# Gathered edges of a graph layer: summed in chunks of 25 tiles through 128-column one-hots, or in units of 16 tiles through 32-column ones

## The reference

```python
h  = x @ node_w.T                       # 12500 x 64
rf = edge_attr_64 @ review_w.T          # 400000 x 64
m  = (h[src] + rf) * edge_weight1
x  = layernorm(x + segment_sum(m, dst, 12500))
```

## Time and profile before

| | before |
|---|---|
| median of 3 runs | 4755.46 us (4745.97 to 4756.59) |
| the profiled execution | 4764.11 us, of which the span from the first to the last instruction is 4762.4 us |
| granted TensorE clock, mean | 0.752 of full speed |
| TensorE busy | 2948.5 us (62%) |
| VectorE busy | 1864.9 us (39%) |
| GpSimd busy | 1996.9 us (42%) |
| ScalarE busy | 1005.4 us (21%) |
| DMA, mean | 39 GB/s |

### The profile page before, as it was taken

One profiled execution on the slowest core, in us unless ns is written; L12 is line 12 of the kernel. 1 busy time (PEld: TensorE's weight loads), 2 busy tenths in 40 slices (PEclk: granted clock), 3 DMA queues, 4 the chain that ended last, 5 costly groups with the idle time before them and its releaser, 6 DMA issues.

```text
span 4762.4 us, 69733 instructions
## 1 busy us (share of the span) xinstructions
PE 2948.5 (62%) x25313; PEld 2219.9 (47%) x25314; DVE 1864.9 (39%) x5496; ACT 1005.4 (21%) x1593; POOL 1996.9 (42%) x2023
## 2 busy tenths in 40 slices
PE   0666666566666666676567566567566576577565
PEld 0444454444444444454445444455355355355345
DVE  2444344334334344344344344344344244344344
ACT  0222122122122122122122122122122122122112
POOL 7334444444444444444444444443443433433541
PEclk9777777677777777777777777677678688677677
DMA  5111211111121211111211212111121111111121
GB/s 102 36 32 39 40 35 39 35 39 35 39 39 34 40 38 36 40 39 34 40 34 39 40 34 39 35 40 37 36 40 37 37 38 38 37 38 38 38 43 33
DMA packets 522588, 186.20 MB, mean 39 GB/s; under 512 B 483570, under 2 KB 490049, under 8 KB 522051
## 3 DMA queue, kind: packets, MB, share of 16 engines
q1 hardware_dynamic: 304936, 74.04, 8.2%
q0 software_dynamic: 64000, 65.66, 7.2%
q10 hardware_dynamic: 153302, 41.80, 4.0%
HBM read 178.15 MB, written 3.20 MB: 38 GB/s over the span
## 4 chain that ended last, share of the span: by engine, by line
PE 56%; another core or an unknown queue 22%; issue 16%; ACT 4%; DVE 2%; DVEq 0%; POOL 0%; ACTq 0%; POOLq 0%
PE count_ps L882 26%; PE x_sums_ps L897 17%; PE window_ps L840 10%; ACT counts L745 4%; DVE hot_lo L497 1%; PE attr_ps L874 1%; PE turn_ps L859 0%; PE turn_ps L856 0%; PE x_sums_ps L906 0%; PE x_sums_ps L905 0%; DVE scatter L442 0%; DVE hot_key L496 0%; DVE x_tab L550 0%; DVE x_tab L563 0%
## 5 line engine op out<-in xcount | busy, mean ns | idle before, releaser
L367 POOL DMA_INDIRECT rows<-x,src x2000 | 1988.2, 994 | 2673.1 <-DMA src<-src 2086.4
L882 PE MATMUL count_ps<-hot_key,hot_lo 128*128 128x343 bf16 x6750 | 1480.6, 373 | 1271.0 <-ACT counts L745 637.9
L882 PEld LDWEIGHTS count_ps<-hot_key,hot_lo 128*128 128x128 bf16 x6750 | 702.1, 115 | 1849.0 <-issue 1068.4
L745 ACT ACTIVATE counts<-count_ps 128x686 f32<-128x686 f32 x1125 | 896.5, 802 | 1952.9 <-remote 1090.7
L496 DVE TENSOR_SCALAR hot_key<-count,cols 128x686 bf16<-128x686 f16 x1125 | 467.3, 415 | 1696.7 <-remote 1031.9
L897 PE MATMUL x_sums_ps<-counts,x_tab 128*64 128x126 f32 (+1 forms) x12348 | 820.9, 282 | 365.7 <-issue 333.4
L897 PEld LDWEIGHTS x_sums_ps<-counts,x_tab 128*64 128x64 f32 x12348 | 732.3, 143 | 439.0 <-issue 395.3
L497 DVE SCALAR_TENSOR_TENSOR hot_lo<-count,cols 128x384 bf16<-128x384 f16 x1125 | 686.4, 610 | 0.0
L442 DVE TENSOR_SCALAR scatter<-column,dst_left,w 128x128 f32<-128x128 f32 x2000 | 523.0, 352 | 254.8 <-PE window_ps L840 237.4
L840 PE MATMUL window_ps<-scatter,rows 128*128 128x128 f32 x4000 | 490.4, 284 | 72.3 <-issue 61.6
L840 PEld LDWEIGHTS window_ps<-scatter,rows 128*128 128x128 f32 x4000 | 475.6, 199 | 92.2 <-issue 89.6
(11 more groups left out here) (112 smaller groups left out, 641.1 us busy)
## 6 DMA issues: line engine op xcount, KB each, us to landing
rows<-edge_attr SPq DMA_DIRECT2D x80, 800.0 KB
g_attr<-edge_attr ACTq DMA_DIRECT2D x62, 576.0 KB, 4.5
rows<-x,src POOLq DMA_INDIRECT x2000
out<-x_tab SPq DMA_DIRECT2D x11, 256.0 KB
counts<-dst SPq DMA_DIRECT2D x1, 1562.5 KB
src<-src SPq DMA_DIRECT2D x80, 12.5 KB, 1.7
dst<-dst SPq DMA_DIRECT2D x80, 12.5 KB
w<-edge_weight SPq DMA_DIRECT2D x80, 12.5 KB
```

Source lines behind the costliest of these rows:

```text
L367: pool.indirect_dma_start(out=rows[:, s, k, 0:F], out_offset=None, in_=x, in_offset=bass.IndirectOffsetOnAxis(ap=src_sb[s][:, k:k + 1].bit ...
L745: act.activation(counts[:, :, t * SPAN:(t + 1) * SPAN].rearrange("p (a h) d -> p a h d", a=2), count_ps[t % 2][:, :, 0:HALF].rearrange("p ...
L882: last = pe.matmul(count_ps[b][:, a, 0:HALF], hot_lo[h][:, i, :], hot_key[h][:, a * HALF:(a + 1) * HALF], start=(i == 0), stop=(i == 2))
```

## The change

Gathered edges are now worked in units of 16 tiles (2048 edges), and all that depends on the loop over windows is gone from the main path.

1. 116 units are gathered (1856 tiles), and 1269 tiles are counted, in 71 groups. A round has ten groups and sixteen units (`STEPS = (2, 1, 2, 1, 2, 2, 1, 2, 1, 2)`), there are seven rounds and no steps behind them, and the last four units stand where the last two chunks stood. The four slots of `rows` hold a unit each.
2. A tile's edges are laid along the partitions in their order. Its one-hot has the 7 nodes that a tile can span, padded to 32 columns, and is the stationary operand: 16 matmuls per unit (32 passes) put each tile's sums on a group of 32 partitions of `unit_ps`, four tiles side by side and four blocks along the bank. ScalarE copies `unit_ps` to SBUF, and four matmuls (8 passes) with a one-hot of 128 partitions x 128 nodes per block, which VectorE makes from each tile's first node, bring the unit into one window of 128 nodes. VectorE adds it at a base read from a table.
3. `src`, `dst` and the weights come in batches of 64 tiles, with a tile on a partition; VectorE subtracts each tile's first node, TensorE turns the batch (7 matmuls) in the middle of `sum_x`, and ScalarE and VectorE copy it. A gather waits for that copy and for the slot, and no longer for a load of its own.
4. A slot is freed by TensorE's last matmul of the unit's sums, and both SyncE's load and GpSimd's gather wait for that, where they waited for VectorE's add before.
5. VectorE's 25 one-hots of 128 x 128 per chunk become two operations of 128 x 112 and one of 128 x 512 per unit.
6. At the start four units (64 tiles) are gathered before the flag is known, where it was four chunks (100 tiles). The tables by chunk are made only where the flag says that all is to be gathered; a table by unit takes their place. The flag now asks the bound of 7 nodes of the gathered tiles too.

```diff
+UT = 16
+SLOTS = 4
+BATCH = 4
+CYCLE = 16
+UNITS = 116
+STEPS = (2, 1, 2, 1, 2, 2, 1, 2, 1, 2)
+LATE_UNITS = 4
+PAD = 32
...
+            def gather_unit(unit):
+                s, c = unit.i % SLOTS, unit.i // BATCH
+                pool.wait_ge(src_ready, unit.b + 1)
+                if not isinstance(unit.u, int) or unit.u >= SLOTS:
+                    pool.wait_ge(unit_summed, unit.u - SLOTS + 1 + BEGUN)
+                pool.sem_inc(gathers_begun, 1)
+                for t in range(UT):
+                    k = unit.i % BATCH * UT + t
+                    pool.indirect_dma_start(
+                        out=rows[:, s, t, 0:F], out_offset=None, in_=x,
+                        in_offset=bass.IndirectOffsetOnAxis(ap=src_cols[:, c, k:k + 1].bitcast(U32), axis=0),
+                    ).then_inc(gathered[s], 16)
...
+            def make_unit_hot(unit):
+                h, k = unit.i % 2, unit.i % BATCH * UT
+                dve.wait_ge(batch_read, unit.b + 1)
+                dve.wait_ge(unit_summed, unit.u - 1 + BEGUN)
+                hot = unit_hot[h][:, :, 0:SPAN]
...
+                dve.tensor_tensor(hot, column[:, 0:SPAN].unsqueeze(1).to_broadcast([P, UT, SPAN]), rel, ALU.is_equal
+                                  ).then_inc(unit_hot_made, 1)
+                dve.wait_ge(unit_hot_made, unit.u * 2 + 1)
+                dve.tensor_tensor(hot, hot, w, ALU.mult).then_inc(unit_hot_made, 1)
...
+            def copy_unit(unit):
+                act.wait_ge(unit_summed, unit.u + 1 + BEGUN)
+                act.wait_ge(unit_multiplied, unit.u - 1 + BEGUN)
+                act.activation(unit_slots[unit.i % 2][:, :], unit_ps[:, :], ACT.Copy).then_inc(unit_copied, 1)
...
+            def sum_unit(unit):
+                s, h = unit.i % SLOTS, unit.i % 2
+                pe.wait_ge(unit_hot_made, unit.u * 2 + 2)
+                pe.wait_ge(attr_landed[s], (unit.b + 1) * 16)
+                pe.wait_ge(gathered[s], (unit.b + 1) * (16 * UT))
+                pe.wait_ge(unit_copied, unit.u + BEGUN)
+                for b in range(BLOCKS_U):
+                    for j in range(QUADS):
+                        t = b * QUADS + j
+                        done = pe.matmul(unit_ps[j * PAD:(j + 1) * PAD, b * 2 * F:(b + 1) * 2 * F],
+                                         unit_hot[h][:, t, :], rows[:, s, t, :], start=True, stop=True)
+                done.then_inc(unit_summed, 1)
+            def multiply_unit(unit, before):
+                pe.wait_ge(unit_copied, unit.u + 1 + BEGUN)
+                pe.wait_ge(slot_hot_made, unit.u + 1)
+                pe.wait_ge(added, before)
+                for b in range(BLOCKS_U):
+                    done = pe.matmul(unit_window_ps, unit_slots[unit.i % 2][:, b * 2 * F:(b + 1) * 2 * F],
+                                     slot_hot[unit.i % 2][:, b, :], start=(b == 0), stop=(b == BLOCKS_U - 1))
+                done.then_inc(unit_multiplied, 1)
...
-                def step_of(g, chunks):
-                    until = sum_chunk(*chunks[0])
+                def step_of(at, turned_batch):
+                    g, units = at.g, at.units
+                    sum_unit(units[0])
                     turn_slots(g - 1)
-                    count_tiles(g)
-                    for chunk in chunks[1:]:
-                        until = sum_chunk(*chunk, until)
-                    multiply_slots(g - 1)
-                    sum_x(g)
+                    wait_attr(g)
+                    if turned_batch:
+                        pe.wait_ge(src_ready, turned_batch.q + 1)
+                    for n, from_ in enumerate(range(0, GT, 2 * HOT_BUFS)):
+                        count_tiles(g, range(from_, min(GT, from_ + 2 * HOT_BUFS)))
+                        if n < len(units):
+                            multiply_unit(units[n], at.added + n)
+                        if n + 1 < len(units):
+                            sum_unit(units[n + 1])
+                    multiply_slots(g - 1, at.added + len(units))
+                    sum_x(g, at.batch)
```

More of the change, by code:

```diff
@@ L21 @@
+from collections import namedtuple
 from contextlib import ExitStack
@@ L287, in round_steps @@
         def round_steps(r):
[L289 removed]
+            i, adds = 0, r * (CYCLE + ROUND_GROUPS) + 1
             for n, size in enumerate(STEPS):
[L291 to L305 removed]
+                units = [unit_at(r, k) for k in range(i, i + size)]
+                begun = [k // BATCH for k in range(i, i + size) if k % BATCH == 0]
+                batch = batch_at(r, begun[0] + 2) if begun else None
+                if isinstance(r, int) and batch and batch.q >= BATCHES:
+                    batch = None
+                yield Step(r * ROUND_GROUPS + n + 1, units, batch, adds)
+                i += size
+                adds += size + 1
@@ L663, in _, with step_of @@
                 begin_hot(1)
-                def step_of(g, chunks):
-                    until = add_chunk(*chunks[0])
-                    make_hot(g, range(HOT_BUFS, GT))
-                    for chunk in chunks[1:]:
-                        until = add_chunk(*chunk, until)
-                    add_slots(g - 1, until)
+                make_unit_hot(unit_at(0, 0))
+                def step_of(at, ahead):
+                    g, units = at.g, at.units
+                    make_slot_hot(units[0])
+                    make_hot(g, range(HOT_BUFS, 2 * HOT_BUFS))
+                    for unit in units[1:]:
+                        make_unit_hot(unit)
+                    make_hot(g, range(2 * HOT_BUFS, 3 * HOT_BUFS))
+                    for unit in units[1:]:
+                        make_slot_hot(unit)
+                    make_hot(g, range(3 * HOT_BUFS, 4 * HOT_BUFS))
+                    add_unit(units[0], at.added)
+                    make_hot(g, range(4 * HOT_BUFS, GT))
+                    for unit in units[1:]:
+                        add_unit(unit, at.added + 1)
+                    for unit in ahead:
+                        make_unit_hot(unit)
+                    if at.batch:
+                        prepare_batch(at.batch)
+                    add_slots(g - 1, at.added + len(units))
                     make_slots_hot(g)
@@ L971, in _ @@
                     multiply_out(early, 0, 1)
-                for c in range(CHUNKS - LATE_CHUNKS, CHUNKS):
-                    until = sum_chunk(*at_slot(c), until)
+                for n, unit in enumerate(last_units):
+                    sum_unit(unit)
+                    if n:
+                        multiply_unit(last_units[n - 1], last_adds + n)
+                multiply_unit(last_units[-1], last_adds + LATE_UNITS)
                 with pe.If(calm_now == 0):
```

633 lines of the change are left out of this document (439 added, 194 removed).

## The result

| | before | after |
|---|---|---|
| median of 4 runs | 4750.72 us (4744.17 to 4756.59) | 4394.43 us (4365.81 to 4404.48) |
| ratio | | 0.9232, 95% interval 0.9186 to 0.9278 |
| the profiled execution | 4764.11 us, span 4762.4 | 4404.48 us, span 4402.7 |
| granted TensorE clock, mean | 0.752 | 0.791 |

The kernel became 356 us faster. The forecast was 4656 us with a range of 4520 to 4850: the sign was right and the size was not.

What follows compares the result with a forecast made beforehand. Bound: TensorE's order of work in quiet time plus time gathers take from it. A round of 307.5 + 43.7 + 3 + 206 + 71 + 8 = 639 us, seven 4473, with start and end 4663, profiled 4665, median 4656; range 4520 to 4850.

Steps and rivals of the forecast that it cites:

- outside the gathers: Per round, 50 us lost behind sixteen gathers, 21 us of old handoffs that stay and 8 us of new ones.
- the handoffs: Between engines, per round: of 30 us, 9.3 of TensorE's idle time goes and 21 stay; 8 us for units' new hops.
- What bounds the kernel: Whole kernel: TensorE's order of work in quiet time, plus the time gathers take from it, 28.4 us per gather before.
- Inside the gathers: GpSimd's 18.75 us gathers, each starting the crawl anew: 206 us lost per round, where 274 were.
- The 6 us behind each gather: TensorE at half clock just after a gather: 3.1 us lost each, 16 times, 50 us per round.
- TensorE's unit: A unit's 32 passes at 0.057 us, 1.82, plus `multiply_unit` 0.91: 2.73 us, 43.7 per round (24 to 73).
- rival 3: In a unit's passes: the four 32-column groups run side by side, 0.9 us or less, total 4555 us; chance 0.15.
- Rounds, counted tiles, VectorE and ScalarE: Seven rounds, 30.75 us per step, 8 groups added; VectorE's and ScalarE's unit work mostly hidden, double steps overrun by 0.9.
- Rival 1: In double steps the second gather gets no fresh start, about 20 matmuls: 154 us more, 4810 us; chance 0.15.
- Rival 2: Inside gathers the crawl is even, 33 matmuls in 18.75 us: a round of 682, total 4957 us; chance 0.08.
- The forecast's last condition: For gathers: if the crawl goes by something else, say the number of instructions or handoffs, shorter gathers buy nothing.

Runs made afterwards that it cites:

- experiment 1: Both kernels without gathers: 2612.89 us before, 2595.62 changed; the changed one with direct DMAs of fixed rows issued by GpSimd, 2602.31, or by SyncE, 2592.05.
- before_none: The kernel before with its gathers left out, slots set to zero once and the x part of the sums left out: 2612.89 us.
- after_none: The changed kernel with no gather, GpSimd only signalling each unit's tiles as landed, the x part of the sums left out: 2595.62 us.
- after_bygroup: The changed kernel with the two loops of a unit's 16 matmuls exchanged, four tiles in a row on one column group: 2746.35 us, chip without slow gathers.
- experiment 4: Changed kernel on a slow-gather chip with gathers of 32 tiles, 4651.63 us; a pause mid-unit, 3842.66; gaps between DMAs, 4110.2; matmul loops exchanged, 4429.84.
- halves2: The changed kernel with three memsets, some 6 us, between each unit's eighth and ninth DMA: 3842.66 us on a slow-gather chip, kernel before 4652.32.
- pairs2: The changed kernel with 56 gathers of 32 tiles in place of 112 of 16: 4651.63 us on a slow-gather chip, kernel before 4652.32.
- before_cut2: The kernel before with two pauses in each gather, behind the eighth and sixteenth of 25 DMAs: 4236.22 us, 0.912 of the kernel before, slow-gather chip.

## Why the prediction was wrong

The profiled execution was 260 us below the sum of 4665. The loop began at 117.9 us (122 forecast). Six rounds took 605.5 us each where the forecast was 639: 201 us. The seventh with the end took 652 where it was 707: 55 us. The step that failed is what the forecast put outside the gathers, and there the handoffs: "21 stay", and 8 more for the new ones. Next to it stands the price of a unit's passes. In the round shown above, 602.3 us long, with each gather cut as the forecast cut it (18.75 us from 4 us behind its first DMA) and each matmul at its quiet price, the terms came out so:

- **What bounds the kernel: right.** Quiet work plus what gathers take; experiment 1 shows both parts, and 2596 us of quiet work leaves little else to be had.
- **Inside the gathers: right.** 202 us per round, where the forecast was 206. The fresh start came out as forecast, 44.7 matmuls in the first 10 us where 33.8 were taken and 10.6 behind them where 12.3 were. That more matmuls mean no smaller loss is because many are a unit's, worth 0.032 us each.
- **The 6 us behind each gather: right.** "3.1 us each, now 16 times, is 50 us", and 47 were measured. In the kernel before the same count gives 3.6 per gather: the 3.1 came off a single stretch and was rather small for it.
- **The handoffs: the term that failed most.** 21 us left and 8 new ones made 29; 11 were measured. The 30 us from which the 21 come were no reading but a remainder, what was left of 28.4 per gather behind all other terms. The kernels without gathers show what was in it:

```profile
77.20:2441.50 2364.30, 2274.28 (x23761) 1848.43 (x23761) 1681.95 (x5020) 943.76 (x1440) 0.00 (x0) 0.99 0.22 44
76.64:2192.80 2116.16, 2058.82 (x24168) 1634.06 (x24168) 1289.19 (x3505) 1008.84 (x1584) 0.00 (x0) 0.99 0.20 44
```

These are six rounds of before_none and six of after_none. A round takes 2364.3 / 6 = 394 us, where the prices add up to 376, and 2116.2 / 6 = 353, where they add up to 342. So 18 us of handoffs per round stood in the kernel before without any gather, and 10 stand in the changed one. The 18 were charged to the gathers: the six rounds of the kernel before take 719.7 us on average, which with 394 of quiet time makes 27.1 lost per gather and not 28.4. The old handoffs that stay and the units' new ones are 10 us together.
- **TensorE's unit: the size was off, and rival 3 had it.** "I take 0.057" for 32 passes, 1.82 us, against 1.02 measured; with `multiply_unit` a unit is 2.0 us and not 2.73, 12 us per round. I ruled side by side out from the two halves of `sum_x`. They alternate between two groups as well, and after_bygroup shows that a row of another shape bore no witness on this. The lower bound "24" of this term was also summed wrong: 16 x (0.91 + 0.91) is 29. What the Trainium skill ("TensorEngine Tiling (Array Packing)", Tiling Modes) says of parallel column groups agrees with the trace in kind: by the factor of up to 4 that the same page gives (Theoretical Speedup) the passes would take an estimated 0.45 us, and the measured factor between the two orders is 2.39 / 1.02 = 2.3. The drain at a change of mode, of which the same section speaks, may show too, and it is small: in after_none 0.205 us lie between the starts of the last matmul of `multiply_unit` and the first of a unit, 0.112 between two of `multiply_unit`, and 0.203 between a unit's last pass and the next matmul. Both stand in the 1.02 and 0.98 us.
- **Rounds, counted tiles, VectorE and ScalarE: right.** 30.75 us per step held, but for the 1 us of handoffs: 71 x 30.75 + 116 x 2.0 + 22 for the batches = 2437 us of TensorE's work, and 2596 with handoffs, start and end.
- **Together** the terms put the round 4 + 3 + 18 + 12 = 37 us below 639, which is the 602 measured; the six rounds were 33.5 below on average. Where a gather is taken to end moves some of the loss from outside to inside, but not its sum: with the end put 4 us behind the start of the last DMA, the whole trace has 13.6 us per unit inside and 2.8 outside (24.4 and 4.2 per gather in the kernel before).
- **Rival 1** didn't come in this round: the second gather of a double step holds 35 to 54 matmuls in its first 10 us, like the first (43 to 56), after 3.2 to 4.7 us of idle time on GpSimd. Over the whole trace it did come in 8 of 40 double steps, where there was next to no gap (experiment 4). **Rival 2** (even crawl) fell as well.
- **The range.** Its lower end, 4520, had rival 3 and little else. The handoffs stood in it as if they were read and not left over. With 58 in place of 79 outside the gathers and 32 us for the units the same sum gives (307.5 + 32 + 3 + 206 + 58) x 7 + 192 = 4438, below the range and 33 us above the execution.

The forecast's last condition, that shorter gathers buy nothing if the crawl goes by something else, was the right question. halves2, pairs2 and before_cut2 answer it: what it goes by is GpSimd's runs of DMAs, by their length above all.

## What to carry to other kernels

Before pricing a change by what an engine does in bad stretches, run or think the kernel without the suspect instruction: here that alone splits 4394 us into 2596 and 1798. What is left over behind all read terms is no term of its own: here 30 us per round of "handoffs" were carried into a new kernel, and a run without gathers shows that 18 of them had nothing to do with the gathers. And where a chip's own behaviour carries most of the time, a version tuned to it (pauses in the gathers) can be 17% faster there and 20% slower on the next chip, so it has to be measured on both.

## What the runs showed of the hardware

- GpSimd's indirect DMAs slow all engines' order of work on some chips and not on others (or in some jobs, since none is known in two): the changed kernel took 4380 and 4394 us in two jobs and 2605 in a third, and the kernel before 4646 to 4778 or 2637 to 2640. An indirect DMA of 128 rows keeps GpSimd busy for 994 ns on the first kind and 1027 on the second. Direct DMAs from GpSimd, as many and of the same bytes, cost 7 us on a chip of the slow kind.
- The slowness grows with the run: 0.70 of the quiet pace in the first 5 us, 0.15 at 10 to 20, 0.05 past 30. The pace starts anew after 6 us without a DMA, and after 3.2 to 4.7 us too, but not after 0.3 to 1.4. With another 0.2 us between DMAs the pace stays at 0.37 up to 25 us. With DMAs of half the rows, 0.04 us closer together, it is 0.05 at 10 to 20 us. What carries it from GpSimd to TensorE is open: DMA is busy for 0.11 to 0.18 there, and plain DMAs don't do it.
- fp32 matmuls with 32-column weights and 128 moving columns run at 0.032 us a pass when neighbours go to different groups of 32 columns, and at 0.075 when most go to the same one.
